# Audio layer on one core: the last stage's first chunk laid between the last attention steps, both stages in one block

## The chip, the cores and the metric

The kernel runs on one core of one Trainium2 chip. The metric is the time of one execution on the device, in microseconds; of several runs the median stands.

## What is computed

An input x of 128 batches, 64 features and 750 samples goes through three parts. Tokens: a window of 8 samples becomes one token by a softmax over the window (94 tokens of 64 features for each batch). Attention: 8 heads of 8 features, whose logits mix q·k, its square and the square of q·k after a QR of q and k; the result is projected and added to the tokens. Feed-forward: a layer norm, a hidden layer of 128, two layers in which a batch pair's own expert (of 16) and a shared one are added, and an output layer, again added. The change touches the end of the second part and the third:

```python
h = h + _L0_attn_ref(_layernorm(h), ...)       # out @ w_proj.T + b_proj, added
hn = (h - mean) / sqrt(var + 1e-5)             # the norm ahead of the feed-forward
f = relu(hn @ Wi.T + bi)
for l in range(2):
    f = relu(Ws[l]-part + Wr[l, route]-part + f)
h = h + f @ Wo.T + bo                          # the output
```

## The kernel before

The 128 batches are held as 64 pairs, a pair on the 128 partitions (two batches of 64 features). Blocks follow each other: `constants`, `pool_project` (tokens, the norm, q, k, v), `orthogonalise` (the QR, the experts' weights), `attend` (attention) and `finish` (projection and feed-forward). A block has one program for each engine, in an order that is written out by hand; engines meet only through semaphores, and each block ends with a meeting of all engines. A wait holds back everything that stands behind it on its engine.

**attend** takes a step for each of the 64 pairs. In a step, TensorE computes the dots (L1061) into three banks `ps_dot`, linear and squared parts of the logits (L1103, `mixing` L1111) into four banks `ps_a`, and for the pair two steps back the product with v (`attended`, L1085) and the softmax's denominators (`denominators`, L1091) into `ps_m`. ScalarE squares the dots (L1164) and takes the exponentials (`exps`, L1156 to L1159). VectorE takes the row maxima (`maxima`, L1187), after a transpose on TensorE (`turn_max`, L1068) the maxima of a head (`heads_max`, L1199 and L1201), which TensorE spreads again (`spread_max`, L1074); then it subtracts them (`shifted`, L1205 to L1212), sums the probabilities' halves (`summed`, L1219) and divides (`output`, L1223 and L1225). GpSimd adds the halves (`halves`, L1009) and builds the operands. The loops end with step 63, and behind it every engine has a tail that finishes pairs 62 and 63. On TensorE it is:

```python
turn_max(PAIRS - 1)
spread_max(PAIRS - 1)
for j in (PAIRS - 2, PAIRS - 1):
    attended(j, j % 2)
    denominators(j)
```

and on VectorE:

```python
maxima(PAIRS - 1)
heads_max(PAIRS - 1)
shifted(PAIRS - 1, 1)
for j in (PAIRS - 2, PAIRS - 1):
    summed(j)
    output(j)
```

ScalarE has `exps` of pair 63 there, GpSimd `halves` of pairs 61, 62 and 63.

**finish** works on 16 chunks of four pairs (376 columns), each of them a chain over the engines: `proj` (TensorE L1318), `add` (VectorE L1418, adds to the tokens), `centred` (TensorE L1324), `square` (ScalarE L1375), `variance` (TensorE L1328), `deviation` (ScalarE L1381, a square root), `normed` (VectorE L1423, a reciprocal, and L1427, a product), `hidden` (TensorE L1336), `hidden_out` (ScalarE L1388), two layers (TensorE L1349, ScalarE L1395 and VectorE L1434), `project_out` (L1357), `residual` (L1413), `turn` (L1363), `rows_out` (L1402) and a store on SP. `select` on GpSimd (L1308) copies the experts' weights of a chunk. The function `staggered` (L670) writes the order: each part has a lag, and in edge c an engine does, in the order of its list, every part for chunk c minus its lag. Six edges are written out, the middle is a loop on the engine (5 passes of two edges), three edges follow. TensorE's list is proj (0), layer 0 (2), turn (3), centred (0), layer 1 (2), variance (0), hidden (1), project_out (2), with the lags in brackets; VectorE's is residual (3), add (0), normed (1), the second layer's relus (2); ScalarE's has square (0), deviation (0) and hidden_out (1). `proj` and `variance` share one PSUM bank, so `proj` of a chunk waits for the deviation of the chunk before. finish's tiles take their own SBUF and all eight PSUM banks.

Of the kernel before, what the change touches and what calls it, by code (L numbers as in the profile page):

```python
# [24 lines left out]
NP = 96  # L25
# [262 lines left out]
def pool_project(nc, x, x_g, x_in, ps_score, tokens, gram, v_dram, qk_dram, top_dram, qk_rows, rows_in, k):  # L288
# [4 lines left out]
    with ExitStack() as ctx:  # L293
# [44 lines left out]
        def _(sp):  # L338
# [15 lines left out]
            def kept_rows(g):  # L354
                for a in range(2):
                    sp.wait_ge(stored[a], 96 * (g + 1))
                sp.dma_start(qk_rows[:, g], qk_dram[span(g, 2 * GP)].rearrange("b j f -> j b f")).then_inc(rows_in[g], 16)
# [337 lines left out]
def orthogonalise(nc, p, gram, m_t, top_dram, qk_dram, qk_rows, rows_in, q_cm, k_cm, k):  # L695
# [10 lines left out]
    with ExitStack() as ctx:  # L706
# [32 lines left out]
        @block.sync  # L739
        def _(sp):  # L740
            sp.dma_start(top[:].rearrange("p n k d -> p (n k d)"), top_dram.rearrange("b m f -> b (m f)")).then_inc(top_in, 16)
            for l in range(LAYERS):
                sp.dma_start(wr_in[:, l, EXP, :], p["Ws"][l, 0]).then_inc(experts_in[l], 16)
                sp.dma_start(wr_in[:, l, 0:EXP, :], p["Wr"][l].rearrange("e o i -> o e i")).then_inc(experts_in[l], 16)

            for g in range(2, NG):
                sp.wait_ge(qk_done, 2 * (g - 1) * (GP // CP))
                sp.dma_start(qk_rows[:, g % 2], qk_dram[span(g, 2 * GP)].rearrange("b j f -> j b f")).then_inc(rows_in[g], 16)
# [120 lines left out]
        def _(pe):  # L869
# [5 lines left out]
            def queries_keys(c, a):  # L875
# [3 lines left out]
                for s in range(2):  # L879
                    for r in range(CP):  # L880
                        for b in range(2):
                            mm = pe.matmul(ps_turn[64 * b:64 * b + 64, 4 + 2 * a + s, NP * r:NP * r + NP],
                                           qk_rows[:, (c * CP // GP) % 2, 2 * (CP * c % GP + r) + b, C * s:C * s + C], k["ident"][0:NP, 0:NP], start=True, stop=True)
# [38 lines left out]
def attend(nc, q_cm, k_cm, m_t, o_cm, v_dram, k):  # L922
# [3 lines left out]
    with ExitStack() as ctx:  # L926
# [28 lines left out]
        BANK = ((1, 0), (2, 3))  # L955
        block = ctx.enter_context(nc.Block())
# [16 lines left out]
        def _(sp):  # L973
# [10 lines left out]
            for i in range(PAIRS):  # L984
                load(i, i % 2)

        @block.gpsimd
        def _(pool):
# [48 lines left out]
            halves(PAIRS - 1, 1)  # L1037

        @block.tensor
        def _(pe):  # L1040
# [102 lines left out]
            for i in range(PAIRS):  # L1143
                step(i, i % 2)
            turn_max(PAIRS - 1)
            spread_max(PAIRS - 1)
            for j in (PAIRS - 2, PAIRS - 1):
                attended(j, j % 2)
                denominators(j)

        @block.scalar
        def _(act):
# [25 lines left out]
            steps(act, step)  # L1178
            for v in range(2):
                exps(PAIRS - 1, 1, v)  # L1180

        @block.vector
        def _(dve):
# [60 lines left out]
            maxima(PAIRS - 1)  # L1244
            heads_max(PAIRS - 1)
            shifted(PAIRS - 1, 1)
            for j in (PAIRS - 2, PAIRS - 1):
                summed(j)
                output(j)


def finish(nc, h, o_cm, out, k):

    sem = nc.semaphore
    with ExitStack() as ctx:
        names = ("proj_done added cent_done squared var_done std_done rstd_done xn_done hid_done hid_out sel_done lay_done "
                 "act_out dve_out wo_done summed turned row_out")
        s = {n: ctx.enter_context(sem("f_" + n)) for n in names.split()}
        stored = [ctx.enter_context(sem(f"out_stored{a}")) for a in range(2)]

        def sb(name, shape):
            return ctx.enter_context(nc.sbuf_tensor(name, shape, F32))

        sq = sb("f_sq", [128, 2, CP, N])
        std = sb("f_std", [128, 2, CP, N])
        xn = sb("f_xn", [128, 2, CP, N])
        hid = sb("hid", [128, 3, 2, CP, N])
        w_sel = sb("w_sel", [128, 2, CP, LAYERS, HID + 1])
        final = sb("final", [128, CP, N])
        rows = sb("rows", [N, 2, CP, 2 * C])  # L1270
        ps = ctx.enter_context(nc.psum_tensor("ps_f", [128, 8, 512], F32))
        block = ctx.enter_context(nc.Block())
        W = CP * N
        STAT_BANK, CENT_BANKS, OUT_BANK = 0, (1, 2), 3
        HID_BANKS, LAYER_BANKS = (4, 5), (4, 6, 5, 7)

        def flat(view):
            return view.rearrange("p r m -> p (r m)")

        def rows_of(bank):  # L1280
            return ps[:, bank, 0:W].rearrange("p (r n) -> p r n", r=CP)

        def pair_of(r):
            return ps[:, LAYER_BANKS[r], 0:2 * N]

        def chunk(t, c):
            return t[:, span(c, CP), 0:N]

        @block.sync
        def _(sp):  # L1290
            def store(c, a):
                sp.wait_ge(s["row_out"], c + 1)
                sp.dma_start(out[span(c, 2 * CP)].rearrange("b n f -> n b f"),
                             rows[:, a].rearrange("n r (b f) -> n (r b) f", b=2)).then_inc(stored[a], 16)

            staggered(sp, NCH, [(0, store)])
            for a in range(2):
                sp.wait_ge(stored[a], 16 * NCH // 2)

        @block.gpsimd  # L1300
        def _(pool):
            def select(c, a):
                if later(c, 2):
                    pool.wait_ge(s["act_out"], 6 * (c - 1))
                    pool.wait_ge(s["dve_out"], 2 * (c - 1))
                for r in range(CP):
                    e = pool.value_load(k["route"][0:1, span(c * CP + r, 1)], min_val=0, max_val=EXP)
                    pool.tensor_copy(w_sel[:, a, r].rearrange("p l f -> p (l f)"),  # L1308
                                     k["ffn_w"][:, bass.ds(e, 1)].rearrange("p e l f -> p (e l f)")).then_inc(s["sel_done"], 1)

            staggered(pool, NCH, [(0, select)])

        @block.tensor
        def _(pe):
            def proj(c, a):
                if later(c, 1):
                    pe.wait_ge(s["std_done"], c)
                pe.matmul(ps[:, STAT_BANK, 0:W], k["w_bd"][:, 3, :], chunk(o_cm, c), start=True, stop=True).then_inc(s["proj_done"], 1)  # L1318

            def centred(c, a):  # L1320
                pe.wait_ge(s["added"], c + 1)
                if later(c, 2):
                    pe.wait_ge(s["xn_done"], c - 1)
                pe.matmul(ps[:, CENT_BANKS[a], 0:W], k["cent_w"][:], chunk(h, c), start=True, stop=True).then_inc(s["cent_done"], 1)  # L1324

            def variance(c, a):
                pe.wait_ge(s["squared"], c + 1)
                pe.matmul(ps[:, STAT_BANK, 0:W], k["mean_w"][:], flat(sq[:, a]), start=True, stop=True).then_inc(s["var_done"], 1)  # L1328

            def hidden(c, a):  # L1330
                pe.wait_ge(s["xn_done"], c + 1)
                if later(c, 1):
                    pe.wait_ge(s["act_out"], 6 * c)
                for b in range(2):
                    q = slice(64 * b, 64 * b + 64)
                    mm = pe.matmul(ps[:, HID_BANKS[b], 0:W], k["wi_bd"][q, b, :], flat(xn[q, a]), start=True, stop=True)  # L1336
                    mm.then_inc(s["hid_done"], 1)

            def layer(c, a, l):
                if l == 0:  # L1340
                    pe.wait_ge(s["hid_out"], 2 * c + 2)
                    if later(c, 1):
                        pe.wait_ge(s["dve_out"], 2 * c)
                for r in range(CP):
                    if l == 0:
                        pe.wait_ge(s["sel_done"], CP * c + r + 1)
                    else:
                        pe.wait_ge(s["act_out"], 6 * c + r + 1)
                    pe.matmul(pair_of(r), w_sel[:, a, r, l, 0:HID], hid[:, l, :, r, :], start=True, stop=True).then_inc(s["lay_done"], 1)  # L1349

            def project_out(c, a):
                pe.wait_ge(s["act_out"], 6 * (c + 1))
                pe.wait_ge(s["dve_out"], 2 * (c + 1))
                if later(c, 1):
                    pe.wait_ge(s["row_out"], c)
                for b in range(2):
                    mm = pe.matmul(ps[64 * b:64 * b + 64, OUT_BANK, 0:W], k["wo_t"][:], flat(hid[:, 2, b]), start=True, stop=True)  # L1357
                mm.then_inc(s["wo_done"], 1)

            def turn(c, a):  # L1360
                pe.wait_ge(s["summed"], c + 1)
                for r in range(CP):
                    mm = pe.transpose(ps[0:N, OUT_BANK, 2 * C * r:2 * C * r + 2 * C], final[:, r, :], k["ident"][:])  # L1363
                mm.then_inc(s["turned"], 1)

            staggered(pe, NCH, [(0, proj), (2, lambda c, a: layer(c, a, 0)), (3, turn), (0, centred), (2, lambda c, a: layer(c, a, 1)),
                                (0, variance), (1, hidden), (2, project_out)])

        @block.scalar
# [171 lines left out]
```

## Time and profile before

| | us |
|---|---|
| median of 3 runs | 901.41 |
| lowest, highest | 899.26, 902.38 |
| the profiled execution: its own time | 901.99 |
| the profiled execution: its span | 900.1 |
| busy in it: PE, DVE, ACT, POOL | 776.0, 708.0, 446.3, 493.2 |

Times in the trace count from the first instruction. About 1.9 us of the execution's own time lie outside of the span. In the trace a float32 matmul is two records, so a chunk's `proj` is "x2". PE is TensorE, DVE VectorE, ACT ScalarE, POOL GpSimd. Where two records of a pipelined engine overlap, the second starts up to 0.1 us before the first one's end.

### The profile page before, as it was taken

To read this page: it belongs to the slowest core of one execution; us is meant where nothing else is said; L and a number is where in the kernel's file an instruction comes from. 1 tells how busy PE (TensorE), PEld (TensorE's weight loads), DVE (VectorE), ACT (ScalarE), POOL (GpSimd) and SP (SyncE) were. 2 spreads that over 40 slices of the span, in tenths; PEclk is the share of its full clock that TensorE was granted. 3 is DMA by queue.
4 is the path that set the end of the run, shared out by engine and by line. 5 is a ranking of instruction groups with operands and counts; after the bars stand their busy time and mean duration, and the time that the engine had idled before them with its cause. 6 is when DMAs were issued, how large, how long until landed. Compare 5 with 4: busy or idle time off the path is not lost. (4 is left out here: it accounts for less than half of the span.)

```text
span 900.1 us, 39670 instructions
## 1 busy us (share of the span) xinstructions
PE 776.0 (86%) x16837; PEld 571.3 (63%) x16837; DVE 708.0 (79%) x1344; ACT 446.3 (50%) x927; POOL 493.2 (55%) x532
## 2 busy tenths in 40 slices
PE   3578888775793699999999999999999998799994
PEld 2244444443673578777788777787877786366663
DVE  4387888885679489988999998999998998376772
ACT  2262424221343166555556655556655555277773
POOL 3242333331000678888888888888888885122220
PEclk9698898987697599999999999999999999599998
DMA  8656662662670122222222222212222220001111
GB/s 298 270 165 194 194 193 57 127 126 58 167 125 1 60 63 63 65 63 76 67 63 63 63 65 71 71 63 63 63 65 78 66 63 23 2 19 29 30 27 34
DMA packets 89197, 77.63 MB, mean 86 GB/s; under 512 B 37145, under 2 KB 79708, under 8 KB 89052
## 3 DMA queue, kind: packets, MB, share of 16 engines
q1 hardware_dynamic: 88524, 73.83, 28.5%
q8 instruction: 131, 2.15, 1.0%
q10 hardware_dynamic: 528, 1.54, 0.5%
q14 instruction: 14, 0.11, 0.0%
HBM read 59.23 MB, written 13.04 MB: 80 GB/s over the span
## 5 line engine op out<-in xcount | busy, mean ns | idle before, releaser
L1164 ACT ACTIVATE sq<-ps_dot 128x376 f32<-128x376 f32 x384 | 165.2, 482 | 152.4 <-PE ps_dot L1061 152.4
L1061 PE MATMUL ps_dot<-q_st,k_blk 64*64 64x94 f32 x6144 | 170.5, 249 | 1.0 <-ACT sq L1164 0.8
L1061 PEld LDWEIGHTS ps_dot<-q_st,k_blk 64*64 64x64 f32 x6144 | 134.6, 134 | 47.5 <-issue 28.9
L557 POOL TENSOR_TENSOR x_g<-x_g,w_odd 128x752 f32<-128x752 f32 x32 | 57.0, 1781 | 107.0 <-ACT w_odd L493 107.0
L994 POOL TENSOR_TENSOR v_blk<-v_rep,vmask 128x384 f32<-128x384 f32 x128 | 106.8, 856 | 10.4 <-PE ps_m L1091 6.4
L1009 POOL TENSOR_TENSOR half<-prob 128x564 f32<-128x564 f32 x64 | 75.7, 1182 | 60.8 <-ACT prob L1159 60.8
L1016 POOL TENSOR_TENSOR k_blk<-k_cm,hmask 128x768 f32<-128x768 f32 x64 | 96.8, 1512 | 1.8 <-PE ps_a L1103 1.8
L1018 POOL TENSOR_TENSOR k_mix<-k_cm,cols 128x768 f32<-128x768 f32 x64 | 96.8, 1513 | 0.0
L1187 DVE TENSOR_REDUCE row_max<-ps_a 128x94 f32<-128x564 f32 x128 | 88.8, 734 | 5.6 <-PE ps_a L1111 5.3
L1111 PE MATMUL ps_a<-sq,mix_w 64*32 64x282 f32 x2048 | 83.0, 406 | 0.5 <-ACT sq L1164 0.5
L1156 ACT ACTIVATE prob<-prob,head_const 128x564 f32<-128x564 f32 x64 | 49.1, 767 | 65.9 <-DVE prob L1209 65.9
L1085 PE MATMUL ps_m<-prob,v_blk 128*64 128x94 f32 x1536 | 78.5, 252 | 1.2 <-DVE q_cm L1225 1.2
L1103 PE MATMUL ps_a<-q_st,k_mix 64*64 64x94 f32 x3072 | 75.4, 243 | 0.7 <-issue 0.4
L1308 POOL COPY w_sel<-ffn_w 128x258 f32 x64 | 25.9, 404 | 89.3 <-DVE hid L1434 60.9
L1085 PEld LDWEIGHTS ps_m<-prob,v_blk 128*64 128x64 f32 x1536 | 66.5, 139 | 8.6 <-issue 1.7
L1103 PEld LDWEIGHTS ps_a<-q_st,k_mix 64*64 64x64 f32 x3072 | 68.0, 134 | 1.3 <-issue 1.1
L386 PE MATMUL ps_spread<-parts,pair_sel 128*128 128x376 bf16 x256 | 59.5, 361 | 10.0 <-POOL parts L467 10.0
L1194 DVE TENSOR_TENSOR k_blk<-ps_m,hmask 128x768 f32<-128x768 f32 x64 | 61.3, 958 | 7.5 <-PE ps_dot L1061 4.9
L493 ACT ACTIVATE w_odd<-ps_spread 128x752 f32<-128x752 f32 x32 | 25.5, 797 | 82.7 <-PE ps_spread L386 82.6
L1002 POOL TENSOR_TENSOR m_blk<-m_t,mask 128x128 f32<-128x128 f32 x64 | 25.9, 406 | 64.0 <-POOLq L706 64.0
L593 DVE TENSOR_REDUCE tokens<-x_g 128x94 f32<-128x752 f32 x64 | 59.0, 924 | 0.5 <-POOL x_g L557 0.5
L1111 PEld LDWEIGHTS ps_a<-sq,mix_w 64*32 64x32 f32 x2048 | 47.2, 106 | 10.3 <-issue 0.9
(215 smaller groups left out, 1454.7 us busy)
## 6 DMA issues: line engine op xcount, KB each, us to landing
v_rep<-v_rows SPq DMA_DIRECT2D x128, 192.0 KB, 3.0
x_g<-in_x_dram SPq DMA_DIRECT2D x15, 1500.0 KB, 6.5
qk_rows_kept<-tok SPq DMA_DIRECT2D x16, 384.0 KB
qk_rows<-qk_rows_kept SPq DMA_DIRECT2D x4, 1536.0 KB, 11.6
v_rows<-tok SPq DMA_DIRECT2D x16, 192.0 KB
q_st<-q_cm SPq DMA_DIRECT2D x64, 47.0 KB, 1.8
out_dram<-rows SPq DMA_DIRECT2D x16, 188.0 KB
x_g<-in_x_dram ACTq DMA_DIRECT2D x1, 1500.0 KB, 7.2
```

The lines of the kernel that those rows point to most:

```text
L386: mm = pe.matmul(ps_spread[:, 2 * (n % 2) + half, 0:HALF], k["pair_sel"][:, half, n, :], parts[:, g % 2, part, :], start=(part == 0), stop ...
L994: vb = pool.tensor_tensor(v_blk[:, a, b].rearrange("p t (o d) -> p (t o) d", o=H), v_rep[:, a, b].rearrange("p (t o d) -> p (t o) d", o=H, ...
L1009: pool.tensor_tensor(half[:], prob[:, a, :, 0:3, :], prob[:, a, :, 3:6, :], ALU.add).then_inc(s["half_done"], 1)
L1016: pool.tensor_tensor(k_blk[:, a, :, 0], k_cm[:, span(i, 1), :].rearrange("p i (u m) -> p (i u) m", m=4).unsqueeze(2).broadcast_to([128, NT ...
L1018: pool.tensor_tensor(k_mix[:, a].rearrange("p t x o -> p (t x) o"), k_cm[:, span(i, 1), :].rearrange("p i m -> p (i m)").unsqueeze(2).broa ...
L1061: mm = pe.matmul(ps_dot[64 * v:64 * v + 64, (2 * g + b) % 3, N * c:N * c + N], k_blk[rows, a, SLOTS * (3 * v + g) + c].rearrange("p k h m ...
L1085: pe.matmul(ps_m[64 * b:64 * b + 64, AV_AT:AV_AT + N], v_blk[:, a, b, t, :], prob[:, a, b, t, :], start=(t == 0), stop=(t == NT - 1), skip ...
L1103: mm = pe.matmul(ps_a[half_of, BANK[b][t // 3], N * (t % 3):N * (t % 3) + N], k_mix[64 * b:64 * b + 64, a, t, 8 * w:8 * w + 8].rearrange(" ...
L1111: mm = pe.matmul(ps_a[32 * c:32 * c + 32, BANK[b][v], 0:3 * N], k["mix_w"][64 * v:64 * v + 64, :], sq[64 * v:64 * v + 64, b, c].rearrange( ...
L1164: act.activation(sq[:, b, :, g, :], ps_dot[:, (2 * g + b) % 3, 0:SLOTS * N].rearrange("p (c n) -> p c n", c=SLOTS), ACT.Square).then_inc(s ...
L1187: dve.tensor_reduce(top[:, b, :], bass.AP(ps_a[:].tensor, 1024 * b, [[4 * 512, 128], [1, N], [512, 2], [N, 3]]), AX.XY, ALU.max).then_inc( ...
L1194: dve.tensor_tensor(k_blk[:, a, :, 1], ps_m[:, KT_AT:KT_AT + NP].rearrange("p (u m) -> p u m", m=4).unsqueeze(2).broadcast_to([128, NT * S ...
```

## The change

attend and finish become one block, without the meeting of the engines between them. finish's norm tiles and `hid` move into `qk_rows` (idle by then, widened from 96 to 128 partitions; its other uses now name rows 0 to 95), its banks into those of `ps_dot` (0 to 2), `ps_a` (3 to 6) and `ps_m` (7). For chunk 0 the parts up to the norm are left out of the staggered order and written into attend's tails by hand. The steady order, its lags and all instructions of chunks 1 to 15 are the same. Two waits are new ahead of chunk 0's `hidden` and first layer, for the banks that attention still reads.

```diff
-                sp.dma_start(qk_rows[:, g], ...)
+                sp.dma_start(qk_rows[0:NP, g], ...)
...
-def attend(nc, q_cm, k_cm, m_t, o_cm, v_dram, k):
+def is_first(c):
+    return isinstance(c, int) and c == 0
+
+def attend(nc, q_cm, k_cm, m_t, o_cm, v_dram, h, spare, out, k):
...
+        free = spare[:].rearrange("p a b f -> p (a b f)")
+        f_sq, std, xn = (free[:, 2 * CP * N * n:2 * CP * N * (n + 1)].rearrange("p (a r n) -> p a r n", a=2, r=CP) for n in range(3))
+        hid = free[:, 6 * CP * N:12 * CP * N].rearrange("p (l b r n) -> p l b r n", l=3, b=2, r=CP)
...
+        def bank_of(n):
+            return ps_dot[:, n, :] if n < 3 else ps_a[:, n - 3, :] if n < 7 else ps_m[:]
...
         # tensor
+            def proj(c, a):
+                if is_first(c):
+                    return
+                project(c)
...
+            def hidden(c, a):
+                if is_first(c):
+                    pe.wait_ge(s["sub_done"], 3 * PAIRS)
...
+            def layer(c, a, l):
+                if l == 0 and is_first(c):
+                    pe.wait_ge(s["out_done"], PAIRS)
...
+            pe.wait_ge(s["squared"], 6 * PAIRS)
+            project(0)
             turn_max(PAIRS - 1)
+            centre(0, 0)
             spread_max(PAIRS - 1)
-            for j in (PAIRS - 2, PAIRS - 1):
-                attended(j, j % 2)
-                denominators(j)
+            attended(PAIRS - 2, 0)
+            denominators(PAIRS - 2)
+            spread_squares(0, 0)
+            attended(PAIRS - 1, 1)
+            denominators(PAIRS - 1)
+            staggered(pe, NCH, [...])
...
         # scalar
+            square_of(0, 0)
             for v in range(2):
                 exps(PAIRS - 1, 1, v)
+            root_of(0, 0)
+            staggered(act, NCH, [...])
...
         # vector
             maxima(PAIRS - 1)
+            add_to(0, 0)
             heads_max(PAIRS - 1)
+            summed(PAIRS - 2)
             shifted(PAIRS - 1, 1)
-            for j in (PAIRS - 2, PAIRS - 1):
-                summed(j)
-                output(j)
+            output(PAIRS - 2)
+            summed(PAIRS - 1)
+            output(PAIRS - 1)
+            norm_of(0, 0)
+            staggered(dve, NCH, [...])
```

`project`, `add_to`, `centre`, `square_of`, `spread_squares`, `root_of` and `norm_of` are the bodies of finish's `proj`, `add`, `centred`, `square`, `variance`, `deviation` and `normed`, with their waits. `select` on GpSimd and the stores on SP follow attention's work on their engines.

## Rows read from the trace of the kernel before

**Rows 1.** The page: granted clock of TensorE in 40 slices of the span.
```profile
PEclk9698898987697599999999999999999999599998
```
**Rows 2.** Busy time by stretch (us and instructions), then granted clock, DMA share, GB/s.
```profile
759.50:761.50 2.00, 0.69 (x3) 0.31 (x4) 1.44 (x3) 0.00 (x0) 0.45 (x1) 1.00 0.00 0
761.50:770.00 8.50, 5.53 (x58) 4.50 (x58) 5.30 (x10) 1.67 (x3) 1.18 (x1) 0.51 0.01 2
770.00:785.50 15.50, 12.01 (x18) 4.01 (x18) 4.18 (x4) 4.13 (x7) 3.23 (x8) 0.50 0.00 2
...
800.00:870.00 70.00, 70.00 (x359) 47.45 (x357) 51.01 (x63) 50.54 (x117) 16.59 (x41) 1.00 0.13 29
```
**Rows 3.** The chain that ended last, from finish's first chunk: start, us, what.
```profile
771.91 0.62 DVE tokens L1418
...
776.42 0.58 ACT f_std L1381
...
779.37 1.63 PE ps_f L1324 x2
...
785.96 1.44 PE ps_f L1349 x8
```
**Rows 4.** Timeline of PE: start, us, instructions, [idle before <-releaser].
```profile
754.77 1.20 PE L1085 MATMUL ps_m<-prob,v_blk 128*64 128x94 f32 x24
755.80 0.33 PE L1091 MATMUL ps_m<-sums,den_w 128*64 128x94 f32 x4
...
757.84 1.28 PE L1111 MATMUL ps_a<-sq,mix_w 64*32 64x282 f32 x32
...
761.44 0.46 PE L1074 MATMUL ps_a<-ident,row_max_e 94*128 94x94 f32 x2 [0.97 <-DVE row_max_e L1201]
...
766.42 2.15 PE L1085 MATMUL ps_m<-prob,v_blk 128*64 128x94 f32 x24 [1.23 <-DVE q_cm L1225]
768.32 0.56 PE L1091 MATMUL ps_m<-sums,den_w 128*64 128x94 f32 x4
770.28 1.59 PE L1318 MATMUL ps_f<-q_cm,w_bd 128*128 128x376 f32 x2 [1.39 <-PEq L926]
...
791.48 0.90 PE L1318 MATMUL ps_f<-q_cm,w_bd 128*128 128x376 f32 x2
```
**Rows 5.** Timeline of DVE over attention's tail and the first norm.
```profile
758.71 1.40 DVE L1187 TENSOR_REDUCE row_max<-ps_a 128x94 f32<-128x564 f32 x2 [0.83 <-PE ps_a L1111]
760.51 0.42 DVE L1199 TENSOR_REDUCE row_max_o<-ps_a 94x16 f32<-94x256 f32 x1 [0.41 <-PE ps_a L1068]
...
763.05 0.80 DVE L1212 TENSOR_TENSOR prob<-ps_a,shift 128x282 f32<-128x282 f32 x2
763.77 0.79 DVE L1219 TENSOR_REDUCE sums<-half 128x188 f32<-128x564 f32 x1
765.24 0.75 DVE L1223 RECIPROCAL inv<-ps_m 128x94 f32<-128x94 f32 x1 [0.68 <-PE ps_m L1091]
...
769.70 0.26 DVE L1225 TENSOR_TENSOR q_cm<-ps_m,inv 128x94 f32<-128x94 f32 x1
...
779.24 2.49 DVE L1423 RECIPROCAL f_std<-f_std 128x376 f32<-128x376 f32 x1
781.76 0.55 DVE L1427 TENSOR_TENSOR f_xn<-ps_f,f_std 128x376 f32<-128x376 f32 x1
```
**Rows 6.** Timeline of ACT: the last exponential, and the table load.
```profile
764.24 0.59 ACT L1159 ACTIVATE prob<-prob,pad_bias 128x376 f32<-128x376 f32 x1
...
774.73 1.28 ACT L1381 ACT_TABLE_LOAD   x1
```
**Rows 7.** Timeline of POOL: the last halves and the first copy of select.
```profile
764.91 1.18 POOL L1009 TENSOR_TENSOR half<-prob 128x564 f32<-128x564 f32 x1 [4.96 <-ACT prob L1159]
771.13 0.40 POOL L1308 COPY w_sel<-ffn_w 128x258 f32 x1 [5.04 <-issue]
```
**Rows 8.** DMA queues from 800 to 870 us: the queue that brings instructions.
```profile
q8 instruction: 1, 0.02, 0.1%
```

More of the change, by code:

```diff
@@ L1144, in _, with project, centred @@
                 step(i, i % 2)
+            def proj(c, a):
+                if is_first(c):
+                    return
+                project(c)
+            def project(c):
+                if later(c, 1):
+                    pe.wait_ge(f["std_done"], c)
+                pe.matmul(bank_of(STAT_BANK)[:, 0:W], k["w_bd"][:, 3, :], chunk(o_cm, c), start=True, stop=True).then_inc(f["proj_done"], 1)
+            def centred(c, a):
+                if not is_first(c):
+                    centre(c, a)
@@ new lines, in centre, with variance, spread_squares @@
+            def centre(c, a):
+                pe.wait_ge(f["added"], c + 1)
+                if later(c, 2):
+                    pe.wait_ge(f["xn_done"], c - 1)
+                pe.matmul(bank_of(CENT_BANKS[a])[:, 0:W], k["cent_w"][:], chunk(h, c), start=True, stop=True).then_inc(f["cent_done"], 1)
+            def variance(c, a):
+                if not is_first(c):
+                    spread_squares(c, a)
+            def spread_squares(c, a):
+                pe.wait_ge(f["squared"], c + 1)
+                pe.matmul(bank_of(STAT_BANK)[:, 0:W], k["mean_w"][:], flat(f_sq[:, a]), start=True, stop=True).then_inc(f["var_done"], 1)
@@ new lines, in residual, with add, add_to @@
+            def residual(c, a):
+                dve.wait_ge(f["wo_done"], c + 1)
+                if later(c, 1):
+                    dve.wait_ge(f["turned"], c)
+                dve.scalar_tensor_tensor(out=final[:], in0=rows_of(OUT_BANK), scalar=k["out_bias"],
+                                         in1=chunk(h, c), op0=ALU.add, op1=ALU.add).then_inc(f["summed"], 1)
+            def add(c, a):
+                if not is_first(c):
+                    add_to(c, a)
+            def add_to(c, a):
+                dve.wait_ge(f["proj_done"], c + 1)
+                dve.scalar_tensor_tensor(out=chunk(h, c), in0=rows_of(STAT_BANK), scalar=k["proj_bias"],
+                                         in1=chunk(h, c), op0=ALU.add, op1=ALU.add).then_inc(f["added"], 1)
@@ L1479, in audio_layer @@
             orthogonalise(nc, p, gram, m_t, top_dram, qk_dram, qk_rows, rows_in, q_cm, k_cm, k)
[L1481 to L1483 removed]
+            attend(nc, q_cm, k_cm, m_t, q_cm, v_dram, tokens, qk_rows, out, k)
 def laid_out(given):
```

280 lines of the change are left out of this document (121 added, 159 removed).

## The prediction

> **What bounds the kernel now.** I began with the slices of the page. TensorE's granted clock is high through attention and dips once more in a late slice [rows 1]; that dip is the place of the change. Busy time by stretch then tells what sets the end from there on: from 800 to 870 us PE is busy for all 70.00 us, at the high level, 2.4 GHz [rows 2]. So finish is bound by TensorE, its steady part holds no slack, and whatever moves its start moves the end by as much. From 761.5 to 785.5 the clock is at the low level, 1.2 GHz, and PE is busy for 5.53 of 8.5 us and 12.01 of 15.5 us. The chain of waits says why: from finish's first projection at 770.28 [rows 4] to past 779.37 one chunk after the other goes PE, DVE, PE, ACT, PE, ACT with nothing beside it [rows 3]. The timelines of the engines show attention's tail ahead of it: its last output ends at 769.70 + 0.26 = 769.96 [rows 5], and the first projection starts 0.32 us later [rows 4].
>
> The figure to follow is the start of `centred` of chunk 1: 779.37 before. Behind it both kernels have the same instructions in the same order (variance, hidden, the first layer at 785.96).
>
> **Removed and moved.** Chunk 0's chain from projection to root fills 770.28 to 776.42 + 0.58 = 777.00, and the meeting of the engines 0.32 us: 7.04 us between attention's end and chunk 1's projection. It moves into gaps of the tail. Eight operations in all: three matmuls, an add, a square, a root with its table load, a reciprocal and a product. The tail, step by step, at the high clock:
>
> PE ends mixing at 757.84 + 1.28 = 759.12 [rows 4]. `project(0)` follows. Its new wait for the last squares costs nothing: mixing itself waited for them. At the high clock it takes 0.90 us [rows 4], so it ends near 760.0 and pushes only the first half of `turn_max`; the second half waits for the second maximum until 758.71 + 1.40 = 760.11 anyway. DVE does `add_to` at 760.1 for 0.62 [rows 3]; behind it stands `heads_max`, which started at 760.51 and now starts near 760.7, **0.2 us late**. Who waits for that is `spread_max`, and `centre(0)` (the same size; some 0.8 us without the overlap of its two records, from 760.75) stands ahead of it but ends about when the maxima are there, at 760.7 + 0.9 = 761.6. Spread until 762.05 (0.46, [rows 4]). `summed(62)`, moved ahead of `shifted`, takes 0.79 from 761.6, so `shifted` begins at 762.35. Before, it ran from about 761.94 until 763.05 + 0.80 = 763.85 [rows 5]; now until 764.25, **0.4 late**. The exponentials end 0.4 later, at 765.2 (764.24 + 0.59 before, [rows 6]), and the last halves on POOL at 766.5 (764.91 + 1.18 before, [rows 7]).
>
> In return `output(62)` no longer waits. Before, it waited for PE's product and denominators at the low clock until 765.24 [rows 5]. At the high clock these take 1.20 and 0.33 [rows 4], 762.05 to 763.6, and output runs from 764.25 to 765.3. `spread_squares` has its squares by 762.1 and runs on PE before 764.5. `attended(63)`: 765.3 to 766.5 (2.15 from 766.42 before). `summed(63)`: 766.5 to 767.3. Denominators 0.33, output 1.04: attention ends at **768.7 instead of 769.96**.
>
> The root stands behind the last exponential: table load 1.28 from 765.2 [rows 6], root 0.58, done at 767.1. Its cover is attention's end at 768.7, with 1.6 us to spare. By the Trainium skill (ScalarE: Activation LUTs, What ACT_TABLE_LOAD costs) a switch of tables costs about 2.66 us with its drain. The trace shows 1.28; by the page the root would end at about 768.5, still under the cover, and the sum would be the same.
>
> `norm_of(0)` then costs its full 782.31 − 779.24 = 3.07 us on DVE [rows 5], and it stands ahead of chunk 1's `add`: queued behind it are the add (0.62, 0.06 of it overlapped) and on PE `centred(1)`. The projection of chunk 1 is done by 768.6, under cover of the norm. So `centred(1)` starts at 768.7 + 3.07 + 0.56 + 0.07 = **772.4**. Before it was 779.37. **Sum: 6.97 us less.** Had the add gone first, about 3.1 us more would come off; the cover of that is gone because the norm was formerly beside PE's work and is now in front of it.
>
> **At nothing.** The three edits of `qk_rows[0:NP]` issue the same transfers. `select` started its copies at 771.13 [rows 7] and can now start after 766.5; chunk 0's first layer needs them more than 6 us behind `centred(1)`. If that cover went, four copies of 0.40 would be the price. The two new waits ahead of chunk 0's hidden and first layer ask for work that ended at 764.25 and 768.7. SP's stores have the same place relative to their rows, and the loads ahead of them are long issued.
>
> **Unknown terms.** First, the clock in the tail. Before, it is 1.00 until 761.5 and 0.51 after; in the two microseconds ahead PE was busy for 0.69 of 2.00 [rows 2]. The change puts 0.90 + 0.8 us of matmul there. I take it that the clock stays high at that point, since PE is now the busier for it. If it falls all the same, `centre` and `spread_max` cost up to 0.8 more, partly under the maxima, and the products take 2.15 and 0.56 [rows 4]: attention ends at 769.7 and 6.0 us come off. Second, the gap on PE from 768.6 to 772.4, 3.8 us, which the change opens. I take the clock as low behind it, as it was before in 770 to 785.5 [rows 2]; it came back 6.1 us after `centred(1)`. With the same sequence I take the same delay. It may come up to 3 us earlier or later (my choice); at half the clock each microsecond loses half of one, so up to 1.5 either way.
>
> The profiled execution took 901.99 with a span of 900.1, so it would be 895.0. The median of the runs is 0.58 lower: 901.41 − 6.97 = **894.4**. A measurement of this kernel can tell about 0.3%, 2.7 us, from no change.
>
> **The rivals.**
>
> *The clock falls in the tail as before.* For it: PE still has gaps, waiting for the maxima and for output. Against: 1.7 us of matmul fill most of the first. 901.41 − 6.0 = 895.4. Chance 0.15.
>
> *The gap on PE costs more than I take.* The clock comes back 3 us later and the tail is late too: 901.41 − 6.0 + 1.5 = 896.9; with a further microsecond of stalls in the added waits, 898. Chance 0.08.
>
> *The gain does not arrive.* The added operations delay `shifted` by as much as they save, by waits that the trace of before does not show: within 2.7 us of 901.4. Against: DVE's rows account for every added operation. Chance 0.04.
>
> *A slower kernel: the loops' instructions are fetched anew.* Place: the five passes of the loop in `staggered`, which now stand elsewhere in each engine's stream, behind attention's. From 800 to 870 the instruction queue brought one packet only [rows 8] and PE had no pause [rows 2], so today nothing is fetched again. If a loop came to lie so that each pass left and came back, two stalls a pass, each as long as PE's wait at the jump into finish, 1.39 us before 770.28, of which the sequencer was the releaser [rows 4]: 10 × 1.39 = 13.9, and 901.41 − 6.97 + 13.9 = 908.3. It decides from 1.4 us a pass (6.97 / 5); under that the kernel is no slower than before. The Trainium skill (Runtime: NRT & Kernel Launch, Instruction fetch mechanics) says that a taken branch whose target isn't in the engine's two pages waits for a fetch. Today's rows show no such wait. Chance 0.03.
>
> **How the numbers follow.** Forecast 0.70; rivals 0.15, 0.08, 0.04, 0.03. The low end takes the forecast with the clock back early (−1.5) and a further microsecond for the spread of the runs shown (899.26 to 902.38): 891.9. The high end takes in the first rival and most of the second: 897.8. Left out are the last two and a little at both ends. Faster 0.70 + 0.15 + 0.08 less a hundredth = 0.92, same 0.05, slower 0.03.
>
> **What would show it.** Right: PE's clock at 1.00 past 761.5 and products of 1.2 us for pair 62; `heads_max` 0.2 late, output of 63 ending near 768.7; the table load between the last exponential and the root, with DVE not waiting for the root; reciprocal and product directly behind output; PE waiting about 4 us for DVE's add before `centred(1)` at 772.4; the high clock back near 778.5; 800 to 870 with PE at 70. Wrong: DVE waiting for the root, `shifted` later than 764.5, a second table load, pauses of PE in the steady loop, or packets of the instruction queue in it.

## The result, and the profile after

The changed kernel takes 891.13 us (median of 4 runs, 890.42 to 893.73); the kernel before, on the same chip and with one more run, 900.46 (899.26 to 902.38). The ratio is 0.9896, 95% interval 0.9868 to 0.9924: 9.3 us less where I had forecast 7.0, and 0.8 us below the low end of the range. The direction was right, the size was not. The interval of the ratio stands for 6.8 to 11.9 us, so this first measurement alone can't tell a gain of 9.3 from one of 7.0. Over all of this study the changed kernel ran 18 times (median 892.6, mean 892.9) and the kernel before 64 times (median 900.7, mean 900.9; with the 12 runs of e1, which are the same kernel, 901.0 for both): 8.0 to 8.4 us. So part of the miss is the first sample, and about 1 us is the prediction's.

The page after has the same shape; the dip of the clock is shorter.

```profile
span 888.6 us, 39660 instructions
PE 764.6 (86%) x16837; PEld 566.0 (64%) x16837; DVE 707.0 (80%) x1344; ACT 446.4 (50%) x927; POOL 492.9 (55%) x532
PEclk9588889897697699999999999999999999799998
```

Busy time by stretch after (columns as in rows 2). In this profile all of attention's tail comes 4.77 us earlier than in the one before (mixing of step 63 ends at 754.35 for 759.12), so the stretches are shifted.

```profile
754.70:756.70 2.00, 1.69 (x7) 0.56 (x5) 1.97 (x5) 0.00 (x0) 0.49 (x1) 1.00 0.00 0
756.70:765.20 8.50, 4.89 (x63) 3.19 (x62) 6.58 (x11) 4.01 (x6) 3.52 (x7) 0.96 0.01 4
765.20:775.00 9.80, 7.11 (x14) 3.18 (x15) 2.75 (x5) 2.20 (x5) 0.81 (x3) 0.51 0.00 0
800.00:860.00 60.00, 60.00 (x308) 40.51 (x306) 43.36 (x54) 42.98 (x99) 14.30 (x36) 1.00 0.13 29
```

The tail now runs at the high clock (0.96 for 0.51 before, [rows 2]), and the steady part is bound by PE as it was: 60.00 of 60 us busy. The low clock lasts from 764.6 to 774.8 instead of 761.6 to 785.5.

PE's timeline after, from the end of step 63:

```profile
753.07 1.28 PE L1166 MATMUL ps_a<-sq,mix_w 64*32 64x282 f32 x32
754.28 0.90 PE L1209 MATMUL ps_dot<-q_cm,w_bd 128*128 128x376 f32 x2
755.02 0.69 PE L1123 MATMUL ps_a<-ident,row_max 128*94 128x128 f32 x2
755.91 0.90 PE L1219 MATMUL ps_dot<-tokens,cent_w 128*128 128x376 f32 x2 [0.20 <-DVE tokens L1434]
...
758.29 0.90 PE L1227 MATMUL ps_dot<-qk_rows,mean_w 128*128 128x376 f32 x2
760.24 1.20 PE L1140 MATMUL ps_m<-prob,v_blk 128*64 128x94 f32 x24 [1.06 <-ACT prob L1290]
762.28 0.38 PE L1146 MATMUL ps_m<-sums,den_w 128*64 128x94 f32 x4 [0.84 <-DVE sums L1396]
762.60 0.90 PE L1209 MATMUL ps_dot<-q_cm,w_bd 128*128 128x376 f32 x2
767.31 1.62 PE L1219 MATMUL ps_dot<-tokens,cent_w 128*128 128x376 f32 x2 [3.82 <-DVE tokens L1434]
```

DVE's:

```profile
753.94 1.40 DVE L1364 TENSOR_REDUCE row_max<-ps_a 128x94 f32<-128x564 f32 x2 [0.83 <-PE ps_a L1166]
755.26 0.60 DVE L1434 SCALAR_TENSOR_TENSOR tokens<-ps_dot,cols,tokens 128x376 f32<-128x376 f32 x1
755.77 0.41 DVE L1376 TENSOR_REDUCE row_max_o<-ps_a 94x16 f32<-94x256 f32 x1
...
756.55 0.79 DVE L1396 TENSOR_REDUCE sums<-half 128x188 f32<-128x564 f32 x1
757.26 0.40 DVE L1382 TENSOR_SCALAR shift<-ps_a,head_const 128x188 f32<-128x188 f32 x1
...
761.43 0.80 DVE L1396 TENSOR_REDUCE sums<-half 128x188 f32<-128x564 f32 x1 [1.33 <-POOL half L1053]
...
763.49 0.26 DVE L1402 TENSOR_TENSOR q_cm<-ps_m,inv 128x94 f32<-128x94 f32 x1
763.67 2.49 DVE L1443 RECIPROCAL qk_rows<-qk_rows 128x376 f32<-128x376 f32 x1
766.19 0.55 DVE L1447 TENSOR_TENSOR qk_rows<-ps_dot,qk_rows 128x376 f32<-128x376 f32 x1
766.66 0.60 DVE L1434 SCALAR_TENSOR_TENSOR tokens<-ps_dot,cols,tokens 128x376 f32<-128x376 f32 x1
```

And ACT's, with the table load between the last exponential and the root:

```profile
758.48 0.77 ACT L1287 ACTIVATE prob<-prob,head_const 128x564 f32<-128x564 f32 x1 [1.15 <-DVE prob L1386]
...
760.16 1.28 ACT L1329 ACT_TABLE_LOAD   x1
761.45 0.58 ACT L1329 ACTIVATE qk_rows<-ps_dot,ln_eps 128x376 f32<-128x376 f32 x1
```

The order is the one that the prediction gave: the projection behind mixing, the add ahead of the heads' maxima, the sum in DVE's former gap, reciprocal and product directly behind the last output with no wait for the root, and PE waiting 3.82 us for chunk 1's add. One thing to note for later: pair 63's product ends at 761.44, but its denominators start at 762.28, 0.84 us later, because DVE's sum waited 1.33 us for POOL's halves. In the new tail the halves set attention's end, not the product.

**How I compare the profiles.** The stages before attention's tail are the same code, but their length varies: the first exponential lies between 312.5 and 316.8 us over the fourteen profiles of this study. So each profile is read from a mark of its own, the start of the exponential that ACT does in step 63 (the last one of the loop; 756.25 in the first profile before, 751.49 after), to three later points. The columns are the first exponential, and then the distance from the mark to the start of the last output's product, to chunk 1's centring, to the last row's eviction, and from centring to eviction:

```
kernel                        first exp.   output 63   centring 1   eviction 15   centring to eviction
before                          316.16       13.45        23.12        134.29        111.17
before, again (e1)              316.16       13.37        23.05        135.43        112.38
after                           312.45       12.00        15.82        127.51        111.69
after, again (e2)               314.98       12.01        15.83        127.02        111.19
after, third (e9)               313.27       12.01        15.83        127.03        111.20
one block only (e3)             315.01       13.36        21.59        133.08        111.48
widened only (e10)              314.23       13.37        23.04        134.25        111.21
sum back (e5)                   314.78       13.24        17.06        129.34        112.28
busy tail in before (e6)        314.03       13.38        23.05        135.45        112.40
gap filled (e7)                 316.83       12.01        15.83        124.85        109.02
add first (e4)                  314.43       12.02        12.84        125.19        112.35
add first, again (e11)          314.36       12.01        12.84        123.67        110.83
add first and filled (e8)       315.95       12.02        12.85        122.63        109.77
add first and filled (e12)      313.73       12.01        12.84        123.62        110.78
```

The columns for output 63 and centring 1 repeat to some 0.1 us in one kernel, so they carry the verdicts; the first one and the last two vary with the moment at which the clock changes.

### The profile page after: what moved, and what is told of

It reads as the page before. It is cut to its first block, busy times and chain, and to the rows that moved or that the text cites. A ratio compares the mean times of both kernels' runs of the same rounds, so it can differ in the third digit from the quotient of the medians.

```text
span 888.6 us, 39660 instructions
## 1 busy us (share of the span) xinstructions
PE 764.6 (86%) x16837; PEld 566.0 (64%) x16837; DVE 707.0 (80%) x1344; ACT 446.4 (50%) x927; POOL 492.9 (55%) x532
## 3 DMA queue, kind: packets, MB, share of 16 engines
q8 instruction: 131, 2.15, 1.0%
## 4 chain that ended last, share of the span: by engine, by line
PE 55%; DVE 7%; issue 1%; ACT 1%; POOL 0%; POOLq 0%; ACTq 0%; DVEq 0%
PE ps_dot L1116 12%; PE ps_a L1166 9%; PE ps_m L1140 8%; PE ps_a L1158 7%; PE ps_a L1252 4%; DVE row_max_o L1376 3%; DVE row_max_e L1378 3%; PE ps_m L1102 3%; PE ps_a L1129 3%; PE ps_a L1123 2%; PE ps_a L1237 2%; PE ps_dot L1209 1%; PE ps_a L1260 1%; PE ps_dot L1219 1%; PE ps_dot L1227 1%
## 5 line engine op out<-in xcount | busy, mean ns | idle before, releaser
L1140 PE MATMUL ps_m<-prob,v_blk 128*64 128x94 f32 x1536 | 76.6, 248 | 1.1 <-ACT prob L1290 1.1
```

The lines of the kernel that those rows point to most:

```text
L1140: pe.matmul(ps_m[64 * b:64 * b + 64, AV_AT:AV_AT + N], v_blk[:, a, b, t, :], prob[:, a, b, t, :], start=(t == 0), stop=(t == NT - 1), skip ...
```

## The experiments

### e1, e2, e9: both kernels again

The difference of the first two profiles is 11.54 us at the last eviction (890.54 against 879.00), but only 6.78 of it lie behind the mark. Is the rest the change's?

> The kernel before, unchanged, measured against itself. What is open is that the profiled pair differs by 11.5 us at the last row's eviction, of which only 6.8 us arise behind attention's last step: 3.7 us stand ahead of the first exponential (316.16 against 312.45) and 1.0 in attention's loop. Theory A (spread of executions: TensorE's clock comes back at another moment in the early stages, 311.0 against 303.8): the ratio is 1.000, and the first exponential of this profile falls anywhere between 311 and 318 us. Theory B (the change speeds up the early stages too): the first exponential is at 316 us, within 1 us, as in the first profile of this kernel.

Measured: 901.91 us, ratio 1.001 (0.9992 to 1.0028). The first exponential at 316.16 again, which spoke for theory B.

> The changed kernel again. Theory A (only the tail and the hand-over are faster; the rest was spread of the executions): ratio 0.9920 to 0.9930, 6.3 to 7.2 us less; in its profile the last step's exponential to chunk 1's centring takes 15.8 us again against 23.1 before, and the first exponential falls anywhere between 311 and 318. Theory B (a gain of 9 to 10 us that is the change's own, part of it ahead of attention's tail): ratio 0.9890 to 0.9900 again, first exponential at 312.5 within 1 us.

Measured: 893.03, ratio 0.9907 (0.9879 to 0.9935), first exponential at 314.98 for 312.45: two profiles of one kernel are 2.5 us apart there, outside of what theory B allowed. The ratio fell between the two theories, and its interval takes in both.

> The changed kernel a third time, on the same chip as the next three. From the last exponential of attention's loop to the last row's eviction it took 127.5 and 127.0 us, against 134.3, 135.4 and (same tail) 135.4; that is 7 to 8.4 us. Theory A (all of the gain lies there; what the medians show beyond it is spread of the earlier stages): ratio 0.9905 to 0.9925, and 126.5 to 128 us in this profile, with the first exponential anywhere between 312 and 317. Theory B (some 1.5 us more are gained ahead of attention's tail): ratio 0.9885 to 0.9900 and the first exponential below 315.1.

Measured: 892.71, ratio 0.9923 (0.9895 to 0.9951), 127.03 us behind the mark, first exponential at 313.27. Together with e10 below (314.23) and e6 (314.03), which have the tail of before, the first exponential does not sort the kernels. The gain behind the mark is 134.86 (mean of before, e1, e6 and e10) less 127.19 (mean of after, e2 and e9) = 7.7 us, and the pooled times differ by 8.0 to 8.4. Theory A is the better one: as far as these times can tell, the gain lies behind attention's last step. Half a microsecond ahead of it they can't rule out.

### e10: the widened tile alone

```diff
-        qk_rows = sb("qk_rows", [NP, 2, 2 * GP, 2 * C])
+        qk_rows = sb("qk_rows", [128, 2, 2 * GP, 2 * C])
```

and rows 0 to 95 named in its three uses, all else as before.

> The kernel before with the one edit that I costed at nothing: qk_rows on 128 partitions, its uses on rows 0 to 95. Theory A: same transfers and matmuls, ratio 1.000 (0.998 to 1.002), first exponential between 312 and 317. Theory B (this edit is what makes the early stages of the changed kernel 1 to 2 us faster): ratio 0.9980 to 0.9985, first exponential below 315.1.

Measured: 899.57, ratio 0.9997 (0.9977 to 1.0018). The edit costs nothing that 12 runs can tell, as predicted. The interval does not rule out theory B's 0.9980 to 0.9985; neither does the first exponential, at 314.23.

### e3: one block, nothing laid in the tail

```diff
-            project(0)
             turn_max(PAIRS - 1)
-            centre(0, 0)
             spread_max(PAIRS - 1)
```

and the same for ACT and DVE; chunk 0 goes through `staggered`, and the sum of pair 62 stands behind the subtraction again.

> The changed kernel with chunk 0 back in the staggered order and the sum of pair 62 back behind the subtraction: one block, but nothing laid between attention's last steps. Theory A: TensorE starts chunk 0's projection right behind the last denominators, without waiting for the last output or the meeting, 1.4 us earlier than before (768.9 for 770.3); VectorE takes the add behind the last output. So chunk 1's centring is 1.4 us earlier relative to the last step (21.7 us behind its exponential for 23.1) and the time 1.4 us lower (ratio 0.9984). Theory B (the merging itself, by the code's or the tiles' new places, is worth more): 3 us or more come off here.

Measured: 900.09, ratio 0.9988 (0.9966 to 1.001): by the time alone it can't be told from no change. The trace can tell it. PE, end of the last denominators and the first projection:

```profile
767.13 0.56 PE L1151 MATMUL ps_m<-sums,den_w 128*64 128x94 f32 x4
767.62 1.62 PE L1214 MATMUL ps_dot<-q_cm,w_bd 128*128 128x376 f32 x2
```

The projection stands right behind the denominators, where before 1.39 us of waiting lay between [rows 4], and the centring comes 1.5 us earlier (21.59 for 23.05 to 23.12), with attention's own end unmoved at 13.36. So the missing meeting, and the projection that no longer waits for the last output, bring 1.5 of the 7.3 us up to the centring. The other 5.8 us are split by e5 below, which has chunk 0 in the tail but the sum in its old place: 21.59 less 17.06 = 4.5 us come with chunk 0 in the tail, and 17.06 less 15.82 = 1.2 us with the sum's new place.

### e5: the sum back in its old place

```diff
-            summed(PAIRS - 2)
             shifted(PAIRS - 1, 1)
+            summed(PAIRS - 2)
```

> The changed kernel with the sum of pair 62 back behind the subtraction. What is disputed is whether the end of attention's tail came 1.44 us earlier by TensorE's clock, as predicted, or by this sum: in the second profile of the kernel before the clock was high for pair 62's product (1.20 us), and its output still started 8.9 us behind the last step's exponential, because the denominators waited for the sum. Theory clock: output of 62 starts 1.0 us later than in the changed kernel, but pair 63 waits for GpSimd's halves and nothing behind it moves: last output 12.0 to 12.1 us behind the last step's exponential, chunk 1's centring 15.8, time as the changed kernel's within 0.3%. Theory sum: last output at 12.5 to 13.0, chunk 1's centring at 16.3 to 16.8, time 0.5 to 1.0 us above the changed kernel's.

Measured: 893.83, ratio 0.9924 (0.9897 to 0.9951); output at 13.24, centring at 17.06 behind the mark. Attention's end is 1.23 us later than in the changed kernel, the way of the sum theory and beyond its upper value of 13.0. By the time alone e5 can't be told from the changed kernel (e9 has 0.9923); the trace carries the verdict. PE's timeline of e5:

```profile
760.32 1.20 PE L1140 MATMUL ps_m<-prob,v_blk 128*64 128x94 f32 x24
763.10 0.38 PE L1146 MATMUL ps_m<-sums,den_w 128*64 128x94 f32 x4 [1.58 <-DVE sums L1396]
763.41 1.56 PE L1227 MATMUL ps_dot<-qk_rows,mean_w 128*128 128x376 f32 x2
764.90 2.15 PE L1140 MATMUL ps_m<-prob,v_blk 128*64 128x94 f32 x24
```

PE has the product of pair 62 done and waits 1.58 us for the sum. So output 62 is late, and pair 63's product, which waits for it, starts 10.10 us behind the mark for 8.75 in the changed kernel. The clock falls at 763.5 in this profile, and that product takes 2.15 us again. The excess over 13.0 goes with this: the sum theory had not counted a slow product.

### e6: the kernel before with its tail kept busy

```diff
+            pe.wait_ge(s["squared"], 6 * PAIRS)
+            pe.matmul(ps_dot[:, 0, 0:4 * N], k["mean_w"][:], k_cm[:, 0:4, 0:N], start=True, stop=True)
             turn_max(PAIRS - 1)
+            pe.matmul(ps_dot[:, 1, 0:4 * N], k["mean_w"][:], k_cm[:, 0:4, 0:N], start=True, stop=True)
             spread_max(PAIRS - 1)
```

> The kernel before with two matmuls of 376 columns put into TensorE's first gaps of the tail, where the changed kernel has chunk 0's projection and centring; their results are not used. Theory clock: the high clock lasts through the tail, pair 63's product takes 1.20 us for 2.15 and its denominators 0.33 to 0.4 for 0.56, so the last output is 12.3 to 12.5 us behind the last step's exponential for 13.4, chunk 1's centring 22.1 for 23.1, and the time about 1 us lower than before (ratio 0.9989). Theory sum (the clock is of no use without the sum's new place): last output at 13.2 or later, time unchanged.

Measured: 900.08, ratio 0.9978 (0.9959 to 0.9996); output at 13.38, centring at 23.05.

```profile
760.30 1.20 PE L1085 MATMUL ps_m<-prob,v_blk 128*64 128x94 f32 x24
763.09 0.58 PE L1091 MATMUL ps_m<-sums,den_w 128*64 128x94 f32 x4 [1.59 <-DVE sums L1222]
764.90 2.15 PE L1085 MATMUL ps_m<-prob,v_blk 128*64 128x94 f32 x24 [1.23 <-DVE q_cm L1228]
```

The clock is high past the gaps that I had named, and it falls behind them, at 762.9, in the wait for the sum. Nothing in the tail moves. That the two matmuls held the clock is not shown: the profile of e1 had the same, the product of 62 at 1.20 us without any added work and the output at 13.37. And e6 does not test what a high clock in pair 63's product would give, since the clock was low again by then. The ratio just excludes 1 although the tail is unchanged; no part of this profile explains it, and it stays open (e1, a kernel against itself, shows 1.001).

### e7: PE's new gap filled

```diff
                 project(c)
+                if isinstance(c, int) and c == 1:
+                    for _ in range(4):
+                        pe.matmul(bank_of(OUT_BANK)[:, 0:W], k["mean_w"][:], chunk(o_cm, 0), start=True, stop=True)
```

and, ahead of PE's `staggered`, a wait for the last subtraction, since the matmuls write into a bank of `ps_a`.

> The changed kernel with four unused matmuls of 376 columns behind chunk 1's projection, in the gap of 3.82 us in which TensorE waits for chunk 1's add. Theory (the gap costs by the clock that it lets fall: centring, variance, hidden and projection then take 1.62 us for 0.90): the clock stays high or falls for a shorter time, centring again at 15.8 us behind the last step's exponential, and from there to the last row's eviction 108 to 109.5 us for 111.2 to 111.7; time 2 to 3 us below the changed kernel's. Rival (the clock falls again at once, or the four matmuls are late and delay the centring): no gain or up to 1 us lost.

Measured: 890.74, ratio 0.9874 (0.9847 to 0.9901).

```profile
769.37 2.69 PE L1207 MATMUL ps_a<-q_cm,mean_w 128*128 128x376 f32 x8
773.36 0.90 PE L1222 MATMUL ps_dot<-tokens,cent_w 128*128 128x376 f32 x2 [1.29 <-DVE tokens L1438]
774.83 0.90 PE L1230 MATMUL ps_dot<-qk_rows,mean_w 128*128 128x376 f32 x2 [0.57 <-ACT qk_rows L1323]
775.66 0.90 PE L1240 MATMUL ps_a<-qk_rows,wi_bd 64*128 64x376 f32 x4
```

The clock does not fall at all before the end of the kernel's work, centring, variance and hidden take 0.90 for 1.62, and centring to eviction takes 109.02 for 111.2 to 111.7: the gap costs 2.2 to 2.7 us through the clock. The median is 1.9 below the pooled 892.6. The Trainium skill (TensorE: Matmul & The Clock Gate, Why this matters for your kernels) advises against idle gaps of PE between bursts; with this gap the trace agrees.

### e4, e11: chunk 1's add ahead of chunk 0's norm

```diff
             output(PAIRS - 1)
+            add_to(1, 1)
             norm_of(0, 0)
```

and `add` leaves out chunk 1.

> The changed kernel with chunk 1's add ahead of chunk 0's norm on VectorE. Theory A (TensorE's wait of 3.8 us for that add is the norm's 3.07 us ahead of it): chunk 1's centring is 3.0 us earlier, 12.8 us behind the last step's exponential for 15.8, TensorE's gap ahead of it is 0.8 us for 3.8, and the time is 3.0 us below the changed kernel's; up to 2 us more if the clock, with the gap gone, falls for a shorter time. Rival (the norm is only moved: chunk 0's hidden layer then waits for it): gain under 1 us, with a wait of TensorE for the product ahead of chunk 0's hidden layer.

Measured: 889.34 (4 runs), ratio 0.9866 (0.9831 to 0.9901), 3.7 below the changed kernel on the same chip (e2, 893.03). PE's timeline of e4:

```profile
765.68 0.90 PE L1209 MATMUL ps_dot<-q_cm,w_bd 128*128 128x376 f32 x2
767.41 0.90 PE L1219 MATMUL ps_dot<-tokens,cent_w 128*128 128x376 f32 x2 [0.82 <-DVE tokens L1434]
768.88 0.90 PE L1227 MATMUL ps_dot<-qk_rows,mean_w 128*128 128x376 f32 x2 [0.57 <-ACT qk_rows L1319]
770.49 1.62 PE L1237 MATMUL ps_a<-qk_rows,wi_bd 64*128 64x376 f32 x4 [0.71 <-DVE qk_rows L1447]
```

The centring comes 2.99 us earlier and the gap is 0.82 us. What is new is 0.71 us of waiting for the product ahead of hidden: with matmuls of 0.90 us, centring and variance are shorter than the norm. The rival is there too, but it takes back 0.7, not 3.

> Chunk 1's add ahead of chunk 0's norm, again, beside the changed kernel and the filled one on one chip. Its first profile had the centring 12.84 us behind the last exponential and 125.2 us from that exponential to the last row's eviction, 2.1 less than the changed kernel's mean of 127.3. I expect 124.5 to 126 and a median 2 us below the changed kernel's; the rival (the norm is only moved) has the median within 1 us of it.

Measured: 889.61, ratio 0.9889 (0.9854 to 0.9923), 123.67 us from the mark to the eviction. In e4 the low clock lasted 6.8 us, in e11 3.4, with the same instructions; the 1.5 us between the two go with that. The median is 3.1 below the changed kernel's on the same chip.

### e8, e12: the add first and the gaps filled

```diff
             spread_squares(0, 0)
+            pe.wait_ge(s["sub_done"], 3 * PAIRS)
+            pe.matmul(bank_of(OUT_BANK)[:, 0:3 * N], k["mean_w"][:], o_cm[:, 0:3, 0:N], start=True, stop=True)
             attended(PAIRS - 1, 1)
+            pe.matmul(bank_of(OUT_BANK)[:, 0:3 * N], k["mean_w"][:], o_cm[:, 0:3, 0:N], start=True, stop=True)
             denominators(PAIRS - 1)
```

and one more behind chunk 1's projection.

> Chunk 1's add ahead of the norm, and three unused matmuls of 282 columns in TensorE's gaps (two around pair 63's product, one behind chunk 1's projection). With the add first alone the centring came 3.0 us earlier, but the clock fell behind the variance, at 770.1, for 6.8 us, and 112.35 us passed from the centring to the last row's eviction. Theory: the three keep the clock high, centring at 12.8 to 12.9 us behind the last step's exponential, 109 to 110 us from there to the end, and the time 2 to 3 us below that of the add first alone, 5 to 6 below the changed kernel's. Rival (hidden of chunk 0 still waits for VectorE's product, and the clock falls in that wait all the same): no gain over the add first alone.

Measured: 890.18, ratio 0.9876 (0.9851 to 0.9900), 122.63 us from the mark. The trace is as expected, the time is not: it is only 0.6 below e7 on the same chip (890.74), though the trace is 2.2 us shorter, and it is not below that of e4.

> Chunk 1's add first and three unused matmuls in TensorE's gaps, again. Its first profile had 122.6 us from the last exponential to the last row's eviction, 4.6 below the changed kernel's, yet its median on another chip was not below that of the add first alone. I expect 122 to 123.5 again, and, with all four on one chip, a median 4 to 5 us below the changed kernel's and 2 to 2.6 below the add first alone. If the medians of the two are within 1 us of each other though the profiles differ by 2.5, the clock stays high in the profiled execution only by chance, and the filled gaps are worth nothing on average.

Measured: 888.36, ratio 0.9866 (0.9835 to 0.9896), 123.62 us. On the chip that e9 to e12 shared, it is 4.4 below the changed kernel (e9) and 1.3 below the add first alone (e11), less than the 2 to 2.6 expected: in e8 the clock did not fall, in e12 it did, for 3.4 us, as in e11. With the add first most of the low clock is gone already, and the unused matmuls add little that these runs can tell. The add first, with or without them, beats both kernels.

## Why the prediction was right and wrong

**Which step failed.** Two did. In the range it is the allowance of 1 us for the spread of the runs. That spread moved the difference of the first two medians from the 8.0 to 8.4 us of all runs to 9.3, and the forecast's base had lain 0.7 too high besides. In the sum it is the account of attention's end: the low clock was taken for what held `output(62)` up, and the sum's new place for a cost of 0.4 us. The runs show that the wait for the sum held it up and that the new place costs 0.1 us. The parts below give the numbers.

**What bounds the kernel** held: PE 60.00 of 60 us in the steady part, and what is won up to chunk 1's centring arrives at the end. The instructions from there on took 111.2 to 111.7 us after and 111.2 to 112.4 before.

**The hand-over** held: from the last output's product to the centring 3.82 us after (763.49 to 767.31) for 9.67 before, 5.85 saved where the terms gave 5.7. The norm costs its full 3.07 us ahead of the add; e4 priced it by itself at 2.99.

**The size of attention's end was near, its cause was wrong.** Predicted 1.26 us, measured 1.44. The failing sentences are "Before, it waited for PE's product and denominators at the low clock until 765.24" and "`summed(62)`, moved ahead of `shifted`, takes 0.79 from 761.6, so `shifted` begins at 762.35". I counted the sum's new place only as a cost of 0.4 us and gave the gain to the clock, which chunk 0's matmuls were to hold up. The kernel before had a row that I did not use, the second one here. The third is the same instruction in e1:

```profile
761.83 2.15 PE L1085 MATMUL ps_m<-prob,v_blk 128*64 128x94 f32 x24
764.61 0.58 PE L1091 MATMUL ps_m<-sums,den_w 128*64 128x94 f32 x4 [0.63 <-DVE sums L1219]
765.06 0.58 PE L1091 MATMUL ps_m<-sums,den_w 128*64 128x94 f32 x4 [1.58 <-DVE sums L1219]
```

The denominators of pair 62 waited for the sum, not for the product. In the four profiles with the tail of before (before, e10, e1, e6) the product of pair 62 took 2.15, 2.01, 1.20 and 1.20 us, the wait for the sum behind it 0.63, 0.77, 1.58 and 1.59, and the last output came at 13.45, 13.37, 13.37 and 13.38. A faster product only lengthened the wait. With the sum early, `output(62)` is not held up, and pair 63's product starts 8.75 us behind the mark (760.24) instead of 10.17 (766.42); in e5, with the sum late, it starts at 10.10. That product also takes 1.20 us now for 2.15, but little of this can count: its denominators waited 0.84 us more, for the halves of POOL. Before, the denominators began 1.90 us behind the start of a product of 2.15 (766.42 to 768.32; these records overlap by 0.25 us, more than the 0.1 us that I had named as usual). Counted from 760.24 that would be 762.14, ahead of the 762.28 at which they started now. With 0.56 us for 0.38 of their own, I estimate that at the low clock attention would have ended some 0.2 us later. In all six profiles with the sum late (e3 and e5 too) the product of pair 63 took 2.15 us, and in all eight with the sum early 1.20, so the clock's own part in the old tail is not shown. Nor was the sum's move tried alone in the kernel before.

The sum costs no 0.4 us: from the start of the maxima the subtraction starts 3.32 us later after (753.94 to 757.26) and 3.23 before (758.71 to 761.94). DVE's sum lies in what was a wait for the spread, and `heads_max` starts 1.83 behind the maxima for 1.80 [rows 5], not 0.2 late. Attention's end gave 0.18 us more than forecast and the hand-over 0.14; together they are the difference between 6.97 and the 7.29 us by which the centring moved.

**The clock behind the gap** was low, as taken. I took one delay for both kernels, the 6.1 us from centring to the high clock in the profile before. The traces show 6.1, 8.9, 8.9 and 6.5 us from centring to the high clock in the four profiles with the tail of before, and 7.5, 6.5 and 6.5 in the three after. The profile that I worked from had the shortest of all; on average centring to eviction is 111.8 before and 111.4 after, 0.4 us more of gain. The bound that I gave this term, 1.5 us either way, covers it.

**The base and the sample.** I took 901.41 from 3 runs; the 64 runs have 900.7. And the first four runs after lie 1.5 us under the 892.6 of all 18. The forecast of 894.4 stands 1.8 above that: 0.7 from the base, 0.3 from attention's end and the hand-over, 0.4 from the clock, and 0.4 unassigned. The range, 891.9 to 897.8, would hold the pooled median; I had allowed 1 us for the sample. The medians of the kernel before on the chips of this study alone lie between 899.87 and 901.91 (12 to 23 runs each), so 1 us was too little for two medians of three or four runs each.

**The rivals.** The clock fell in the gap, not in the tail. The gap costs 2.2 to 2.7 us (e7), and that was in the forecast already. The gain arrived: no added operation delayed the subtraction by more than 0.1 us. The loops were not slowed: PE is busy for 60.00 us of 800 to 860, and that stretch had no packet on the instruction queue at all. The table load took 1.28 us and the root started 0.01 us behind it; the 2.66 us with a drain that the Trainium skill (ScalarE: Activation LUTs, What ACT_TABLE_LOAD costs) gives did not show here. Neither value would have mattered.

**What stays open**: the 0.2% of e6; the 0.4 us unassigned above; what the sum's new place brings alone, and with the clock held high in the old tail; and how much the unused matmuls are worth on average beside the add first.

## What to carry to other kernels

When a step gets out of a wait, look for what it waited for in both places. A slow matmul and, behind it, a wait for another engine's short sum can add up to the same time at either clock; the releaser of that wait tells which of the two to move. In a hand-over between two stages, first lay the next stage's head into the gaps, then order what is left by who waits for it: an add of 0.6 us that feeds the bound engine belongs ahead of a norm of 3.1 us that is not needed yet. Read small changes from a mark within the trace, near the edit, and leave the early stages out.

## What the runs showed of the hardware

- Before, the clock fell at 761.6 although PE had made no pause of 1 us: it was busy for 0.69 of the 2 us ahead, in three pieces [rows 2]. In e10, with the same tail, it fell at 759.6, and in e5 and e6 during or behind a wait of 1.6 us.
- The same instructions had the low clock for 6.8 us in one execution and 3.4 in another (e4, e11), for 3.4 us or not at all (e12, e8). In the kernel before it fell at 761.6 in one profile, so that pair 62's product took 2.15 us, and at 764.9 in another (e1), with 1.20; attention ended at the same place to 0.1 us.
- The executions of the kernel before spread from 895.33 to 906.64 us over 64 runs, more than the change is worth; and the first exponential of one and the same kernel lay at 312.45, 314.98 and 313.27 us.
